# Cross-attention with a mixture of experts: clearing, query projection and two loads in another order

## The chip, the cores and the metric

The kernel runs on one core of one Trainium2 chip. The metric is the device time of one execution in microseconds (us), from the first to the last instruction of the core. Each kernel is run several times and the median is compared. The execution that the profiler recorded is one more run, and its own time stands below.

## The reference

For each of 32 batches, 100 query tokens attend to 1,444 context rows of 128 numbers, with 16 heads of 8 numbers each. The result is added to the tokens, and then each token goes through the best two of eight experts. The mask holds only ones.

```
x    = x + attention(layernorm(x), ctx, ctx, mask, W_q, W_k, W_v, W_o)     # x [32,100,128], ctx [32,1444,128]
       scores = clip(q @ k.T / sqrt(8), -50, 50);  p = exp(scores);  out = (p @ v) / sum(p)
x    = x + sum over the best 2 of 8 experts of weight * (gelu(layernorm(x) @ w1[e]) @ w2[e])
```

All of it is in float32.

## The kernel before

**Stages.** There is a start, 32 batches of attention, and a stage for the experts. The batches 0 and 1 are written out, the batches 2 to 29 are a loop over pairs (`Fori(1, B // 2 - 1)`, an even batch and then an odd one), and the batches 30 and 31 are written out again. Every engine has its own program with its own loop, so each pair ends on every engine with a branch.

**A batch.** The scores of a batch are made in 20 chunks of 3 or 2 units (a unit is 128 context rows of one group of four heads, 128x400 numbers). In a chunk TensorE (PE) multiplies `k_stack` by `q_stack` into PSUM (`score_chunk`, L816), ScalarE (ACT) takes exp (L1058), VectorE (DVE) clips (L1214), and PE later multiplies the values by the probabilities (`weigh_values`, L828). The chunks alternate between two areas of PSUM, so the scores of chunk c + 1 wait for the exp of chunk c - 1. The tables `STEP_AT` and `HALF_AT` say behind which chunk each other step stands: the next batch's keys (L747) and values (L756), and the steps of the batch before towards the experts. In chunk 15 PE does 24 multiplications in a row with the values, 48 rows of the trace under L828; this piece of each batch (x48) serves below as a mark for the length of a batch.

**Stacked keys and queries.** Keys and queries are split into a high and a low part (`k_hi`, `k_lo`, `q_parts`) and spread over the partitions by DMAs between SBUF places: `k_stack` in thirds of four DMAs of 256 KB, from SyncE's queue (SP, L509), `q_rep` and `q_stack` in DMAs of 50 KB, in the start from ACT's queue too. `q_stack` holds zeros between its blocks, which GpSimd (POOL) writes once (L641).

**The start.** DVE and POOL normalise the first four batches of x; PE turns the first context and these tokens, projects the first third of the keys (`first_key(0)`), then the queries (`project_q`), then the other keys and the values. DVE splits the queries ahead of the keys. The first scores wait for all of `q_stack` and for the first third of `k_stack`.

**Loads from HBM.** x comes in three parts (`X_PARTS`); the last, 16 batches in 1,600 rows of 512 bytes, is issued by ACT at the end of the start. A context is loaded by `load_blocks(b, p)` (L979) on ACT's queue: 128 partitions times 45 rows of 128 bytes, 5,760 small rows, 720 KB, into one of two buffers; four more rows come from SP. DVE turns a context for the next batch in three pieces behind chunks 0, 7 and 11 (`turn_keys`, L1145). There are 30 of these loads. Each stands at the head of `attend` on ACT, ahead of the batch's first exp:

```
def attend(b, p):
    if not (isinstance(b, int) and b + 2 >= B):
        ...
        load_blocks(b + 2, p)
    for c in range(CHUNKS):
        act.wait_ge(scores_ready, CHUNKS * b + c + 1)
```

[...] The functions, with the line numbers of the profile:

Of the kernel before, what the change touches and what calls it, by code (L numbers as in the profile page):

```python
# [48 lines left out]
def xattn_moe(nc, x, ctx, mask, W_q, W_k, W_v, W_o, gate_w, w1, w2, out):  # L49
    B, SQ, D = x.shape  # L50
# [21 lines left out]
    KSTEPS = TILES // KC  # L72
# [46 lines left out]
    TURN_AT = [0, 7, 11]  # L119
    WEIGHED = 5  # L120
    SPLIT_AT = 15

    ALONE = [("value", k) for k in range(KSTEPS)]

# [13 lines left out]
    FIRST_STEPS = [[s for _, s in steps] for steps in PLANS]  # L138
# [3 lines left out]
    X_PARTS = [slice(0, QB), slice(QB, 4 * QB), slice(4 * QB, B)]  # L142
# [5 lines left out]
    def is_first(b):  # L148
        return isinstance(b, int) and b < 2
# [4 lines left out]
    def scratch_step(b, n):  # L154

        return ITS_BASE[b] + n if is_first(b) else len(STEPS) * b + BEFORE + n
# [8 lines left out]
    def planned(b, c):  # L165

        if is_first(b):
            return [(FIRST_STEPS[b][n], n) for n in range(len(PLANS[b])) if FIRST_AT[b][n] == c]
        last = isinstance(b, int) and b == B - 1
        steps = [n for n in range(len(STEPS)) if STEP_AT[n] == c and (not last or IN_LAST[n])]  # L170
        return [(STEPS[n], sum(IN_LAST[:n]) if last else n) for n in steps]
# [16 lines left out]
    def turns_before(b):  # L188

        return KSTEPS * (b - 1) if not isinstance(b, int) or b >= 2 else 0  # L190
# [9 lines left out]
    def later(b, least=1):  # L200

        return not isinstance(b, int) or b >= least
# [7 lines left out]
    with es:  # L210
        def sb(name, shape, dt=F32):
            return es.enter_context(nc.sbuf_tensor(name, shape, dt))
# [4 lines left out]
        def sem(name):  # L217
            return es.enter_context(nc.semaphore(name))
# [3 lines left out]
        x_all = sb("x_all", [SQ, B, D])  # L222
# [107 lines left out]
        x_loaded = [sem(f"x_loaded{h}") for h in range(3)]  # L330
# [3 lines left out]
        ctxT_ready = sem("ctxT_ready")  # L334
# [28 lines left out]
        scratch_filled = sem("scratch_filled")  # L363
# [71 lines left out]
        def score_banks(c):  # L435

            first = SB0 * (c % 2)
            return scores[:, first:first + UNITS[c], 0:GQ]

        def probs_of(c):  # L440

            first = FIRST_UNIT[c] % RING_UNITS
            return probs[:, first:first + UNITS[c], :]
# [172 lines left out]
        def _(pool):  # L616
# [15 lines left out]
            def invert_deviations(r):  # L632
                part = slice(r * QB, (r + 1) * QB)
                pool.wait_ge(moments_ready, r + 1)
                nc.gpsimd.tensor_scalar(rstd[:, part], moments[:, part, 1], EPS, None, ALU.add).then_inc(var_ready, 1)
                pool.wait_ge(var_ready, r + 1)
                nc.gpsimd.tensor_tensor(rstd[:, part], rstd[:, part], half[:, part], ALU.pow).then_inc(rstd_ready, 1)

            invert_deviations(0)
            for p in range(2):  # L640
                nc.gpsimd.memset(q_stack[p][:].bitcast(F32), 0.0).then_inc(q_stack_cleared, 1)  # L641
            pool.wait_ge(ctx_turned, KSTEPS)
            nc.gpsimd.memset(ctx_cols[0][:, WHOLE * Q:BLOCKS * Q], 0.0).then_inc(spare_keys_cleared[0], 1)
            invert_deviations(1)
# [17 lines left out]
            for r in range(DVE_NORMS, QSTEPS):  # L662
                invert_deviations(r)
                pool.wait_ge(rstd_ready, r + 1)
                for j in range(QB):
                    b = r * QB + j
# [71 lines left out]
        def _(pe):  # L738
# [7 lines left out]
            def project_k(into, k):  # L746
                return nc.tensor.matmul(into[:, 0:KEYS[k]], w_turned[:, WK, :], ctxT[:, KEY_COLS[k]],  # L747
                                        start=True, stop=True)

            def project_q(into):  # L750
                return nc.tensor.matmul(into[:, 0:NQ], w_turned[:, WQ, :], xT, start=True, stop=True)  # L751
# [96 lines left out]
            turn_tokens(o_sum, 0).then_inc(xT_in_psum, 1)  # L848
            turn_rows(scores[:, 2, :], 0, 2).then_inc(ctx_turned, 1)
            pe.wait_ge(w_turned_ready, 1)  # L850

            def first_key(k):

                pe.wait_ge(ctxT_ready, k + 1)
                project_k(scores[:, FIRST_KEYS_IN[k], :], k).then_inc(keys_projected, 1)

            first_key(0)
            pe.wait_ge(xT_ready, 1)
            project_q(scores[:, 1, :]).then_inc(q_in_psum, 1)
            first_key(1)  # L860
            first_key(2)
            for step, (name, k) in enumerate(ALONE):
# [113 lines left out]
        def _(act):  # L976
            def load_blocks(b, p):

                act.dma_start(ctx_cols[p][:, 0:WHOLE * Q].rearrange("p (t d) -> p t d", d=Q),  # L979
                              ctx[b, 0:WHOLE * Q, :].rearrange("(i t) (g d) -> g i t d", t=WHOLE, d=Q)  # L980
                              ).then_inc(ctx_loaded[p], 16)
# [54 lines left out]
            for step, (name, k) in enumerate(ALONE):  # L1036
# [4 lines left out]
                                   ).then_inc(scratch_emptied[step % 2], 1)  # L1041
                if k == 0:
                    first_stack()
            act.dma_start(x_all[:, X_PARTS[2], :], x[X_PARTS[2]].rearrange("b q d -> q b d")).then_inc(x_loaded[2], 16)

            def attend(b, p):
                if not (isinstance(b, int) and b + 2 >= B):
                    if later(b, 2):
                        act.wait_ge(ctxT_ready, turns_before(b) + KSTEPS)
                    elif b == 1:  # L1050
                        act.wait_ge(scratch_filled, scratch_step(0, FIRST_STEPS[0].index(("turn", KSTEPS - 1))) + 1)
                    load_blocks(b + 2, p)
                for c in range(CHUNKS):
                    act.wait_ge(scores_ready, CHUNKS * b + c + 1)
                    if later(b) or c >= RING:

                        act.wait_ge(pv_done, HALVES * b + 2 * last_tile_under(c) + 2)
                    nc.scalar.activation(probs_of(c), score_banks(c), ACT.Exp, scale=SCALE).then_inc(exp_ready, 1)  # L1058
                    for (name, k), n in planned(b, c):
                        take(name, k, b + 1, b - 1, scratch_step(b, n), scratch_use(b, n)[0])  # L1060
                    if c == GATED + 2 and later(b):
                        second_share(b - 1)

            attend(0, 0)
            attend(1, 1)
            with act.Fori(1, B // 2 - 1) as i:
                attend(2 * i, 0)
                attend(2 * i + 1, 1)
            attend(B - 2, 0)
            attend(B - 1, 1)  # L1070
            for n, (name, k) in enumerate(FINISH):
# [35 lines left out]
        def _(dve):  # L1107
# [30 lines left out]
            def turn_keys(i, p, b, k):  # L1138

                if k == 0:  # L1140
                    dve.wait_ge(ctx_loaded[1 - p], 16 * (i + 1 + p))
                    dve.wait_ge(ctx_over_loaded[1 - p], 16 * (OVER * (i + p) + 1))
                dve.wait_ge(scratch_filled, value_turned(b - 1, k) + 1)
                cols = slice(KEY_BLOCKS[k].start * Q, KEY_BLOCKS[k].stop * Q)
                nc.vector.transpose(ctxT[:, cols], ctx_cols[1 - p][:, cols]).then_inc(ctxT_ready, 1)  # L1145
# [165 lines left out]
            def attend(i, p, b):  # L1311
                for c in range(CHUNKS):
# [10 lines left out]
                    for k in range(KSTEPS):  # L1323
                        if c == TURN_AT[k] and later(b) and not (isinstance(b, int) and b + 1 >= B):
                            turn_keys(i, p, b, k)
                    if c == SPLIT_AT and not (isinstance(b, int) and b + 2 >= B):
                        split_queries(b + 2)
# [137 lines left out]
```

## Time and profile before

| | |
|---|---|
| median of 3 runs | 1036.55 us (1033.01 to 1038.11) |
| the profiled execution | 1029.2 us, its span 1027.4 us |
| busy: PE, DVE, ACT, POOL | 93%, 79%, 70%, 33% of the span |
| the chain that ended last | PE 88%, DMA 2%, ACT 2%, issue 2%, SP's queue 2%, DVE 1%, POOL 1%, ACT's queue 1% |
| mean granted clock of TensorE | 0.969 of full speed |

The busy shares are averages over stages. The chain is followed back from the last instruction to what released each step, so a row of it is time that the end waited for. "ACTq" and "SPq" are the sequencers of ACT and SP, where a DMA is issued; a row there is the time that the issue held the sequencer, not the transfer. The timeline's bracket behind a row is how long the engine sat idle before it, and what ended that.

### The profile page before, as it was taken

Reading aid. Unit: us, or ns where it says so; the run is one execution under the profiler, and the core shown is the slowest. Engines: PE = TensorE matmul, PEld = TensorE weight load, DVE = VectorE, ACT = ScalarE, POOL = GpSimd, SP = SyncE. Lnnn points to the kernel's source line nnn. Section 1 sums busy time; section 2 is a strip of 40 time slices with the busy share of each in tenths; the row PEclk is TensorE's granted clock in tenths of the full one; section 3 lists DMA queues with packets and bytes.
Section 4 is the critical chain, followed back from the end, with each engine's and each line's share of the span. In section 5 each row is a group of like instructions: output and inputs, shape, how many; then the busy total and the mean of one; then the engine's idle time right before and its main releaser. Section 6 shows DMA issues by size and latency. Waiting matters only on the chain.

```text
span 1027.4 us, 31365 instructions
## 1 busy us (share of the span) xinstructions
PE 953.8 (93%) x9974; PEld 695.5 (68%) x9975; DVE 808.5 (79%) x2140; ACT 716.0 (70%) x941; POOL 340.0 (33%) x422
## 2 busy tenths in 40 slices
PE   3799999999999999999999999999999996599980
PEld 2566666666666666666666666666666773599980
DVE  5477888888888888888888888888888985444433
ACT  2577878787878787878787878787878774244430
POOL 3182322222222222222222222222222234255554
PEclk9699999999999999999999999999999999699995
DMA  6755666666666666666666666666666663122216
GB/s 182 182 150 173 186 189 188 186 188 189 186 188 186 189 187 189 186 189 188 187 186 189 186 189 186 189 186 187 189 188 186 184 229 86 41 66 67 66 43 191
DMA packets 312438, 172.70 MB, mean 168 GB/s; under 512 B 205274, under 2 KB 260518, under 8 KB 312406
## 3 DMA queue, kind: packets, MB, share of 16 engines
q1 hardware_dynamic: 131898, 142.19, 42.4%
q10 hardware_dynamic: 175612, 23.48, 14.5%
q0 software_dynamic: 4896, 6.63, 2.1%
q8 instruction: 17, 0.28, 0.1%
q14 instruction: 15, 0.12, 0.0%
HBM read 36.83 MB, written 22.08 MB: 57 GB/s over the span
## 4 chain that ended last, share of the span: by engine, by line
PE 88%; DMA 2%; ACT 2%; issue 2%; SPq 2%; DVE 1%; POOL 1%; ACTq 1%; POOLq 0%; DVEq 0%
PE scores L816 32%; PE o_sum L828 28%; PE scratch L747 7%; PE scratch L756 7%; PE scores L940 5%; PE scores L951 5%; ACT probs L1058 2%; SPq L604 1%; DMA q_stack<-q_rep 1%; ACTq L979 1%; PE scratch L794 1%; DMA x_all<-in_x_dram 1%; PE scratch L751 0%; DMA q_and_ctx<-expert_outputs 0%; POOL rows L688 0%
## 5 line engine op out<-in xcount | busy, mean ns | idle before, releaser
L1058 ACT ACTIVATE probs<-scores 128x800 f32<-128x800 f32 (+1 forms) x640 | 603.8, 973 | 152.2 <-PE scores L816 139.8
L816 PE MATMUL scores<-q_stack,k_stack 128*128 128x400 f32 x1536 | 412.9, 385 | 15.2 <-DMA q_stack<-q_rep 9.2
L1214 DVE TENSOR_SCALAR probs<-probs 128x800 f32<-128x800 f32 (+1 forms) x640 | 402.4, 661 | 16.9 <-ACT probs L1058 11.8
L816 PEld LDWEIGHTS scores<-q_stack,k_stack 128*128 128x128 f32 x1536 | 250.8, 190 | 140.8 <-ACT probs L1058 84.1
L828 PE MATMUL o_sum<-probs,v_both 128*17 128x200 f32 x6144 | 304.0, 335 | 0.0
L828 PEld LDWEIGHTS o_sum<-probs,v_both 128*17 128x17 f32 x6144 | 158.4, 97 | 109.3 <-issue 39.9
L699 POOL DMA_INDIRECT expert_rows<-rows,row_atu x64 | 71.9, 1124 | 322.0 <-DVE row_atu L1301 290.2
L756 PE MATMUL scratch<-w_turned,ctxT 128*128 128x128 f32 x768 | 101.0, 275 | 0.0
L756 PEld LDWEIGHTS scratch<-w_turned,ctxT 128*128 128x128 f32 x768 | 99.7, 191 | 0.7 <-issue 0.3
L747 PE MATMUL scratch<-ctxT,w_turned 128*128 128x512 f32 x186 | 85.3, 567 | 0.0
L1154 DVE COPY v_both<-scratch 128x512 f32<-128x512 f32 x93 | 63.7, 685 | 20.4 <-PE scratch L756 20.4
L725 POOL DMA_INDIRECT expert_outputs<-ctx_nat,tile_home x57 | 55.7, 977 | 64.4 <-DVE ctx_nat L1415 61.7
L688 POOL TENSOR_SCALAR rows<-token,moments,rstd 100x128 f32<-100x128 f32 x64 | 70.7, 1107 | 6.9 <-POOL rstd L684 6.9
L682 POOL TENSOR_SCALAR rstd<-moments 100x1 f32<-100x1 f32 x32 | 32.3, 1011 | 114.7 <-DVE moments L1254 114.6
L1018 ACT COPY k_full<-scratch 128x512 f32<-128x512 f32 (+1 forms) x93 | 52.1, 561 | 19.2 <-PE scratch L747 14.3
L1118 DVE TENSOR_TENSOR k_lo<-k_full,k_hi 128x512 fp32r<-128x512 f32 (+1 forms) x93 | 61.5, 662 | 3.2
L940 PE MATMUL scores<-ctxT 128*128 128x128 f32 x456 | 62.2, 281 | 0.0
L951 PE MATMUL scores<-w_sb,k_full 128*128 x456 | 61.6, 279 | 0.0
L1088 ACT ACTIVATE k_full<-scores 128x512 f32<-128x512 f32 x57 | 34.1, 598 | 38.6 <-PE scores L940 38.0
L940 PEld LDWEIGHTS scores<-ctxT 128*128 128x128 f32 x456 | 57.1, 197 | 0.3 <-issue 0.2
L1116 DVE CAST k_hi<-k_full 128x512 fp32r<-128x512 f32 (+1 forms) x93 | 38.0, 409 | 24.3 <-ACT k_full L1018 24.2
L951 PEld LDWEIGHTS scores<-w_sb,k_full 128*128 128x128 f32 x456 | 56.3, 194 | 0.3 <-issue 0.2
(148 smaller groups left out, 665.7 us busy)
## 6 DMA issues: line engine op xcount, KB each, us to landing
k_stack<-k_hi SPq DMA_DIRECT2D x192, 256.0 KB, 3.5
k_stack<-k_lo SPq DMA_DIRECT2D x192, 256.0 KB, 4.8
expert_rows<-fill SPq DMA_DIRECT2D x32, 406.2 KB
q_and_ctx<-in_ctx_dram ACTq DMA_DIRECT2D x15, 720.0 KB
ctx_nat<-in_ctx_dram ACTq DMA_DIRECT2D x15, 720.0 KB
q_rep<-q_parts SPq DMA_DIRECT2D x126, 50.0 KB
q_stack<-q_rep SPq DMA_DIRECT2D x126, 50.0 KB, 2.6
v_both<-expert_rows SPq DMA_DIRECT2D x57, 65.0 KB, 1.8
```

The costliest lines, as they stand in the source:

```text
L688: ins = nc.gpsimd.tensor_scalar(rows[:, k, TOKEN:D], token[:], moments1[:, 0:1], rstd1[:, 1:2], ALU.subtract, ALU.mult)
L699: nc.gpsimd.indirect_dma_start(out=expert_rows[0:E * CAP, :], out_offset=bass.IndirectOffsetOnAxis(ap=row_atu[:, k:k + 1], axis=0), in_=ro ...
L747: return nc.tensor.matmul(into[:, 0:KEYS[k]], w_turned[:, WK, :], ctxT[:, KEY_COLS[k]], start=True, stop=True)
L756: last = nc.tensor.matmul(scratch[:, j * P:(j + 1) * P], ctxT[:, t * P:(t + 1) * P], w_turned[:, WV, :], start=True, stop=True)
L816: last = nc.tensor.matmul(score_banks(c)[:, m, :], k_stack[p][:, g, t * P:(t + 1) * P], q_stack[p][:, :, g, :], start=True, stop=True)
L828: last = nc.tensor.matmul(sums_of(g, s), v_ones[p][:, t, 2 * g + s, :], probs[:, u, s * PQ:(s + 1) * PQ].rearrange("p (h q) -> p h q", h=2 ...
L940: last = nc.tensor.matmul(hidden_in[n % 2][:, c * P:(c + 1) * P], w1_tile[:, n % 2, c * P:(c + 1) * P], tileT[:, n % 2, :], start=True, st ...
L951: last = nc.tensor.matmul(y_in[n % 2], hiddenT[:, n % 2, c, :], w2_sb[:, bass.ds(expert, 1), c, :].rearrange("f o d -> f (o d)"), start=(c ...
L1058: nc.scalar.activation(probs_of(c), score_banks(c), ACT.Exp, scale=SCALE).then_inc(exp_ready, 1)
L1118: nc.vector.tensor_tensor(k_lo[:, cols], k_full[:, k, 0:KEYS[k]], k_hi[:, cols].bitcast(F32), ALU.subtract).then_inc(k_split, 1)
L1154: nc.vector.tensor_copy(v_ones[p][:, k * KC:(k + 1) * KC, :, 0:2 * DH], scratch[:, bank, :].rearrange("p (t n d) -> p t n d", t=KC, n=PAIR ...
L1214: nc.vector.tensor_scalar(chunk, chunk, LOW, HIGH, ALU.max, ALU.min).then_inc(probs_ready, 1)
```

## The change

- POOL clears both `q_stack` buffers before it inverts the first deviations, not after.
- PE projects the first queries ahead of the first third of the keys. It waits for a second copy of context (`ctxT_ready` 2) first, since the queries go into the PSUM bank that this copy reads.
- ACT issues the last part of x and the load of the third context (number 2) behind the exp of chunk 3 in batch 0, not before batch 0.
- The loads at the head of each batch are gone. Behind the exp of chunk 14, batch b now loads context b + 3 into the buffer that batch b has just turned; it waits for that batch's third turn (in batch 0 for the last turn in PSUM).
- ACT's loop is one pair shorter, and batches 28 and 29 are written out on ACT.
- DVE waits for the four extra rows of a context ahead of the third turn, not of the first.

```
+    LOAD_AT = 14
+    LATE_X_AT = 3
...
-            invert_deviations(0)
             for p in range(2):
                 nc.gpsimd.memset(q_stack[p][:].bitcast(F32), 0.0).then_inc(q_stack_cleared, 1)
+            invert_deviations(0)
...
             pe.wait_ge(w_turned_ready, 1)
+            pe.wait_ge(ctxT_ready, 2)
...
-            first_key(0)
             pe.wait_ge(xT_ready, 1)
             project_q(scores[:, 1, :]).then_inc(q_in_psum, 1)
+            first_key(0)
...
-            act.dma_start(x_all[:, X_PARTS[2], :], x[X_PARTS[2]].rearrange("b q d -> q b d")).then_inc(x_loaded[2], 16)
...
             def attend(b, p):
-                if not (isinstance(b, int) and b + 2 >= B):
-                    if later(b, 2):
-                        act.wait_ge(ctxT_ready, turns_before(b) + KSTEPS)
-                    elif b == 1:
-                        act.wait_ge(scratch_filled, scratch_step(0, FIRST_STEPS[0].index(("turn", KSTEPS - 1))) + 1)
-                    load_blocks(b + 2, p)
                 for c in range(CHUNKS):
...
                     nc.scalar.activation(probs_of(c), score_banks(c), ACT.Exp, scale=SCALE).then_inc(exp_ready, 1)
+                    if not later(b) and c == LATE_X_AT:
+                        act.dma_start(x_all[:, X_PARTS[2], :], x[X_PARTS[2]].rearrange("b q d -> q b d")).then_inc(x_loaded[2], 16)
+                        load_blocks(2, 0)
+                    if c == LOAD_AT and not (isinstance(b, int) and b + 3 >= B):
+                        if later(b):
+                            act.wait_ge(ctxT_ready, turns_before(b + 1) + KSTEPS)
+                        else:
+                            act.wait_ge(scratch_filled, scratch_step(0, FIRST_STEPS[0].index(("turn", KSTEPS - 1))) + 1)
+                        load_blocks(b + 3, 1 - p)
...
-            with act.Fori(1, B // 2 - 1) as i:
+            with act.Fori(1, B // 2 - 2) as i:
                 attend(2 * i, 0)
                 attend(2 * i + 1, 1)
+            attend(B - 4, 0)
+            attend(B - 3, 1)
...
                     dve.wait_ge(ctx_loaded[1 - p], 16 * (i + 1 + p))
+                if k == KSTEPS - 1:
                     dve.wait_ge(ctx_over_loaded[1 - p], 16 * (OVER * (i + p) + 1))
```

On POOL in the start, before and then after the change (`rstd` is the inverted deviation, `q_and_ctx` holds the first context buffer):

```order
L628 AFFINE_SELECT ident<-ident 128x128
L635 TENSOR_SCALAR rstd<-moments 100x4
L637 TENSOR_TENSOR rstd<-rstd,half 100x4
L641 MEMSET q_stack 128x1600 x2
L643 MEMSET q_and_ctx 128x32
```

```order
L630 AFFINE_SELECT ident<-ident 128x128
L642 MEMSET q_stack 128x1600 x2
L637 TENSOR_SCALAR rstd<-moments 100x4
L639 TENSOR_TENSOR rstd<-rstd,half 100x4
L645 MEMSET q_and_ctx 128x32
```

The two memsets moved ahead of the two operations on `rstd`.

On ACT from the end of the start to chunk 5 of batch 0, before and then after (each ACTIVATE is the exp of one chunk; the copy into `ctxT` belongs to chunk 3):

```order
L1039 COPY v_both<-scratch 128x32x16 x2
L1044 DMA x_all<-in_x_dram 100x16x128
L979 DMA q_and_ctx<-in_ctx_dram 128x45x32
L1058 ACTIVATE probs<-scores 128x1200
L1058 ACTIVATE probs<-scores 128x800
L1058 ACTIVATE probs<-scores 128x1200
L1058 ACTIVATE probs<-scores 128x800
L1014 COPY ctxT<-scratch 128x512
L1058 ACTIVATE probs<-scores 128x1200
```

```order
L1042 COPY v_both<-scratch 128x32x16 x2
L1054 ACTIVATE probs<-scores 128x1200
L1054 ACTIVATE probs<-scores 128x800
L1054 ACTIVATE probs<-scores 128x1200
L1054 ACTIVATE probs<-scores 128x800
L1056 DMA x_all<-in_x_dram 100x16x128
L982 DMA q_and_ctx<-in_ctx_dram 128x45x32
L1017 COPY ctxT<-scratch 128x512
L1054 ACTIVATE probs<-scores 128x1200
```

The two loads moved from ahead of the first exp to between the fourth and the fifth, ahead of a copy.

On ACT at the entry of the loop before the change, and then behind chunk 14 of the loop's even batch after it (the last ACTIVATE of the first fence is chunk 0, the first of the second is chunk 14):

```order
L1058 ACTIVATE probs<-scores 128x800
L1066 UNCONDITIONAL_BRANCH
L1066 ISA
L979 ISA
L979 DMA q_and_ctx<-in_ctx_dram 128x45x32
L1054 ISA
L1057 ISA
L1058 ACTIVATE probs<-scores 128x1200
```

```order
L1054 ACTIVATE probs<-scores 128x1200
L1060 REGISTER_ALU
L982 ISA
L982 DMA ctx_nat<-in_ctx_dram 128x45x32
L1011 REGISTER_ALU
L1020 REGISTER_ALU
L1021 COPY k_full<-scratch 128x512
```

The load moved from between the last exp of one batch and the first of the next to between the exp of chunk 14 and the copies of the next batch's keys.

## Rows read from the trace of the kernel before

**Rows 1.** Chain in order of time, the start: start us, us, what.

```profile
9.42 3.39 DVE probs L1183 x4
...
13.99 1.05 PE scores L747 x2
...
19.61 0.61 SPq L509
...
20.98 8.47 DMA q_stack<-q_rep
```

**Rows 2.** Timeline of POOL and DVE: start us, us, engine, line, operation [idle before].

```profile
8.00 0.24 POOL L635 TENSOR_SCALAR rstd<-moments 100x4 f32<-100x4 f32 x1 [5.52 <-DVE moments L1176]
...
9.35 2.79 POOL L641 MEMSET q_stack<- 128x1600 f32 x2
...
23.28 1.15 DVE L1183 TENSOR_SCALAR w_sb<-x_all,moments,rstd 100x128 f32<-100x128 f32 x4 [0.31 <-POOL rstd L637]
```

**Rows 3.** Page, DMA issues: times, KB each, median us to landing.

```profile
k_stack<-k_lo SPq DMA_DIRECT2D x192, 256.0 KB, 4.8
```

**Rows 4.** Timeline of ACT and its queue, start and batch 0.

```profile
20.66 0.70 ACTq L1044 DMA_DIRECT2D x_all<-in_x_dram  x1
...
21.39 3.55 ACTq L979 DMA_DIRECT2D q_and_ctx<-in_ctx_dram  x1
...
37.18 0.59 ACT L1014 COPY ctxT<-scratch 128x512 f32<-128x512 f32 x1 [1.58 <-PE scratch L742]
...
54.61 1.17 ACT L1058 ACTIVATE probs<-scores 128x1200 f32<-128x1200 f32 x1 [0.38 <-PE scores L816]
```

**Rows 5.** One window: us, busy PE, PEld, DVE, ACT, POOL, PEclk, DMA, GB/s.

```profile
25.20:41.50 16.30, 9.54 (x35) 7.17 (x39) 6.98 (x25) 6.73 (x9) 2.06 (x3) 0.50 0.85 210
```

**Rows 6.** Timeline of ACT and PE's weight loads, into an even batch.

```profile
556.03 0.56 ACTq L979 DMA_DIRECT2D q_and_ctx<-in_ctx_dram  x1
556.78 3.25 ACT L1058 ACTIVATE probs<-scores 128x1200 f32<-128x1200 f32 x3 [0.47 <-issue]
...
558.00 0.48 PEld L816 LDWEIGHTS scores<-q_stack,k_stack 128*128 128x128 f32 x3 [0.45 <-ACT probs L1058]
```

**Rows 7.** Chain in order of time: x48 of batches 18, 19, 20, 29, 30.

```profile
525.43 2.15 PE o_sum L828 x48
...
550.90 2.15 PE o_sum L828 x48
...
576.77 2.16 PE o_sum L828 x48
...
807.77 2.15 PE o_sum L828 x48
...
833.03 2.15 PE o_sum L828 x48
```

**Rows 8.** Timeline of SP's queue and ACT, into an odd batch.

```profile
529.84 0.62 SPq L509 DMA_DIRECT2D k_stack<-k_hi  x1
...
530.00 0.84 ACT L1058 ACTIVATE probs<-scores 128x800 f32<-128x800 f32 x1 [0.16 <-PE scores L816]
...
530.15 0.55 ACTq L979 DMA_DIRECT2D ctx_nat<-in_ctx_dram  x1
```

**Rows 9.** Timeline of DVE, ACT and PE's weight loads, chunk 14 of batch 19.

```profile
546.09 0.64 DVE L1145 STREAM_TRANSPOSE ctxT<-q_and_ctx 128x448 f32<-128x448 f32 x1
...
548.45 1.18 ACT L1058 ACTIVATE probs<-scores 128x1200 f32<-128x1200 f32 x1 [0.60 <-PE scores L816]
549.66 1.21 ACT L1018 COPY k_full<-scratch 128x512 f32<-128x512 f32 x2
...
550.47 0.14 PEld L798 LDWEIGHTS scratch<-ident,rows 100*128 100x128 f32 x1
```

**Rows 10.** DMA view, packets on ACT's queue (q10): 530.2 to 553.9, then 31 to 60.

```profile
q10 hardware_dynamic: 5764, 0.74, 19.8%
...
q10 hardware_dynamic: 5843, 0.77, 18.5%
```

## The prediction

> **What bounds the kernel now.** I read the chain that ended last first: 88% of it is PE, so a change elsewhere helps only where the chain leaves PE. It leaves it in two places that this change touches. The first is the start. In the chain in order of time [rows 1] the normalisation on DVE takes 3.39 us, and a DMA into `q_stack` takes 8.47 us and ends at 29.45; only then do the first scores begin. The window behind it [rows 5] shows what that idle time leaves: from 25.2 to 41.5 us TensorE's granted clock was 0.50, the lower of its two levels, 1.2 GHz, and PE was busy for 9.54 of 16.3 us. The second place is the step from one batch into the next. From x48 to x48 [rows 7] the step into batch 19 costs 25.47 us, into batch 20 25.87, and into batch 30, where ACT issues no load and no loop branches, 25.26. So each even step has 0.61 us too much and each odd one 0.21, and the timeline shows where: ACT's first exp of batch 20 was ready but came 0.47 us late for "issue", and PE's weights waited 0.45 us for that exp [rows 6].
>
> My sum is made against the profiled execution's own 1029.2 us (span 1027.4, and 1.8 around it). The median shown is 1036.55, which is 7.3 more; I take the sum off the median.
>
> **The change part by part.**
>
> *POOL's clearing.* Four normalisations took 3.38 us in the start and 1.15 later, with the same shapes [rows 2]; only the first four lie beside the memsets of 9.35 to 12.14. The memsets move into POOL's idle 5.52 us ahead of 8.00, which covers their 2.79, and the `rstd` steps are not delayed. Gain on the chain: 3.39 - 1.15 = 2.2 us. Without that cover, `rstd` would be late by up to 2.8 and the gain gone.
>
> *Queries first.* The first key piece, 1.05 us on PE [rows 1], leaves the queries' path. PE now waits for the copy of the turned tokens, which that piece had covered, but PE turns the last context rows meanwhile. The added wait for the second context copy costs nothing: ACT makes that copy ahead of the tokens' copy, for which PE waits anyway; the keys and values queue behind both. The keys now end 1.05 behind the queries, but DVE splits the queries first, as before, so not all of the 1.05 is lost to the keys; I take a gain of 0.4 for them (bounds 0 and 1.05). SP's issues, the key thirds and then `q_stack`, come 2.2 + 0.4 = 2.6 earlier.
>
> *The two loads out of the start.* They leave ACT's queue at 20.66 and 21.39 [rows 4], beside the 8.47 us transfer. What lands last then? The fourth DMA of the key third was issued at 19.61 [rows 1], now at 17.0, and takes a median 4.8 us [rows 3]: 21.8. `q_stack` goes out at 18.4 and has one third ahead of it, as always. I take 21.9 in place of 29.45: **-7.5 us**, of which 2.6 is from the earlier issues. The landing could stay at 8.47 if the key thirds and not the loads hold it (-2.6), or follow the issue in 2.6 (-8.5); I take nearly the shorter, since the loads are the only traffic there that other landings don't have.
>
> *The same loads in batch 0.* Now ACT's sequencer issues them between two exps. The one took 0.70 and the other 3.55 [rows 4], 4.3 together. In the trace ACT was free from 35.60 (37.18 less 1.58) until PE's turned context came; the issues start while the exp of chunk 3 runs, about 0.8 earlier (an exp of two units takes 0.84 [rows 8]), so they end near 39.1 on the old clock face and hold the copy and the exp of chunk 4 by **+1.9 us**. Bounds: nothing, if the second issue needs only the 0.55 of the loop [rows 8], since 1.3 is covered; 4.3, if nothing is. The part of x is asked for by DVE five chunks later; if it were late, the clips and then PE's values would wait.
>
> *The fourth context.* Chunk 14 of batch 0 stands at 54.61, some 20 us behind the exp of chunk 3 [rows 4], and there ACT issues the next load on a queue that holds x and the third context. A context in the loop is all moved between 530.2 and 553.9, 5,764 packets [rows 10], 23.7 us; x has to go ahead of it. So the issue meets a queue that is not empty. It need not wait for the landing: the issue at 21.39 got through by 24.94, though the 5,843 packets of 31 to 60 us [rows 10] are the context's 5,760 and 83 others, so x still moved then. I take **+2.0 us**, bounds 0 and 9 (the context's 23.7 and for x about 5, an estimate from the 3.55 for which it held the next issue, against 20). Behind it on ACT stand the copies of two key thirds, and behind these PE's later steps of the chunk.
>
> Start together: -7.5 + 1.9 + 2.0 = **-3.6 us**.
>
> *The loads at chunk 14 in the loop.* Into batch 20 ACT branches and issues for 0.56 us, and the exp comes 0.47 late [rows 6]; without the issue the branch ends under the exp of chunk 19, and PE gets back its 0.45. Even steps in the loop: 14 (batches 2 to 28), 6.3 us. Into an odd batch the issue of 0.55 lies under the exp of 0.84 [rows 8]; what it costs is within the 0.21 of that step, and I take 0.15, as the loop's register instructions have a share. Odd steps: 15 (batches 1 to 29), 2.2 us. Together **-8.5**; bounds -3.5 (even 0.25, odd 0) and -11.7 (0.61 and 0.21 in full).
>
> At chunk 14 I cost the issue at nothing. What hides it is the exp of 1.18 us that starts at 548.45; the copies follow at 549.66 [rows 9], and an issue of 0.55 is over by then. The wait in front of it is for the third turn, which ends at 546.73, 1.7 us before. If that cover failed, the first copy would end 0.55 later than about 550.27, and PE, which loads the next weights at 550.47, would wait. The transfer itself keeps its pace of one per batch and lands earlier than it is needed.
>
> *The rest.* DVE's moved wait releases a turn that waited for nothing in the trace; nothing. Two more batches written out on ACT save one branch, too little to count.
>
> Sum: -3.6 - 8.5 = **-12 us**, from 1029.2 to 1017 in a profiled run and from 1036.55 to **1024.5** in the median.
>
> **The rivals.**
>
> *A, the start gives nothing back.* The issues in batch 0 cost only their covered 0.7 and 0.55, and PE's shorter idle time leaves the clock at its upper level. For it: an issue alone takes 0.55. Against: 3.55 was measured behind this very load of x, and PE still idles before the first scores. Then -7.5 - 8.5, and up to 2 of the half-clock stretch (at the upper level its 9.54 us of PE would be 4.8, most of it beside ACT's exps): about 1018.5 to 1020.5.
>
> *B, the start gives all back.* The issue at chunk 14 of batch 0 waits until the third context has nearly landed, +7 rather than +2: start +1.4, sum -7, 1029.5. For it: 20 us are less than the transfers need. Against: x had not landed when the issue behind it got through.
>
> *C, the branch stays.* PE's and ACT's branches alone hold the even step, and the loop gains 3.5: -7, 1029.5. For it: the even step's excess has both causes mixed. Against: the row names ACT's issue as what PE's weights waited for.
>
> *D, slower.* The issue at chunk 14 does not fit under the exp. In each of 29 batches (0 to 28) the copies, the next exp and PE come 0.55 later: +16, sum +4, 1040.5. It decides from 0.41 us a batch on. Against it: an issue of ACT at 530.15 took the usual 0.55 although SP issued from 529.84 to 530.46 [rows 8]. The Trainium skill (Perfetto Trace Analysis, section DMA Instruction — HWDGE (DVE, Sync)) says that an issue first locks a descriptor generator that the issuing sequencers share and holds it until all its descriptors are made, which would speak for D where SP's issues meet chunk 14; by that rule one issue of SP in the way would add about 0.6 a batch, an estimate. The row at 530.15 does not show such a lock; the 3.55 behind x may.
>
> **How the numbers follow.** Under or over by 0.5%, 5.2 us, is about what this measurement can tell from no change, so faster means below 1031.4. Chances: my forecast (1020.5 to 1028.5) 0.50, A 0.14, B 0.22, C 0.08, D 0.06. The forecast and A are faster; so are some 0.7 of B and C, which end near the border; the rest of them and a milder D are the same. Faster 0.83, same 0.12, slower 0.05. The range reaches from A's clock case to B and C: 1017 to 1031.
>
> **What would show it.** In the profile after: four normalisations in about 1.2 us near 9.4; first scores near 22; the two issues behind the fourth exp and the time that they take; how long the issue at chunk 14 of batch 0 takes; no "issue" wait ahead of the first exp of an even batch, and periods from x48 to x48 near 25.3 for odd and 25.4 for even batches; copies of the keys right behind the exp of chunk 14. I would be wrong if the loop's issue stretched beyond that exp (D), if batch 0 grew by more than 4 us, or if the first scores stayed later than 25.

## The result

| | before | after |
|---|---|---|
| median of 4 runs each | 1037.33 us (1033.01 to 1041.27) | 1065.26 us (1060.1 to 1065.89) |
| ratio, with its 95% interval | | 1.026 (1.021 to 1.031): slower |
| the profiled execution, its span | 1029.2, 1027.4 us | 1060.1, 1058.3 us |
| busy: PE, DVE, ACT, POOL | 93%, 79%, 70%, 33% | 91%, 76%, 67%, 31% |
| mean granted clock | 0.969 | 0.960 |

The change costs 28 us in the median, 31 in the profiled executions. In the changed kernel L982 is `load_blocks`, L1021 the copy of a key third, L818 the scores, L830 the values (x48), L1054 the exp.

The start up to the first scores went as forecast. Timeline of PE in the changed kernel, first for the start, then around chunk 14 of batch 14:

```profile
22.01 1.15 PE L818 MATMUL scores<-q_stack,k_stack 128*128 128x400 f32 x5 [2.84 <-DMA q_stack<-q_rep]
...
437.19 0.43 PE L800 MATMUL scratch<-ident,rows 100*128 100x100 f32 x1 [3.85 <-ACT k_full L1021]
437.55 3.55 PE L830 MATMUL o_sum<-probs,v_both 128*17 128x200 f32 x48
...
464.22 2.23 PE L830 MATMUL o_sum<-probs,v_both 128*17 128x200 f32 x48
```

The first scores stand at 22.01; `q_stack` had held them until 29.45 [rows 1]. But at 437.19 PE waits 3.85 us for ACT's copy of a key third, a wait that the kernel before does not have. ACT's timeline names the cause; in it "issue" is idle time that no wait in the profile explains, and the ACTq row just ahead shows ACT's sequencer held for that time:

```profile
26.14 0.32 ACTq L1056 DMA_DIRECT2D x_all<-in_x_dram  x1
26.48 3.34 ACTq L982 DMA_DIRECT2D q_and_ctx<-in_ctx_dram  x1
...
29.86 0.59 ACT L1017 COPY ctxT<-scratch 128x512 f32<-128x512 f32 x1 [2.50 <-PE scratch L744]
...
48.56 1.17 ACT L1054 ACTIVATE probs<-scores 128x1200 f32<-128x1200 f32 x1 [0.39 <-PE scores L818]
48.56 5.84 ACTq L982 DMA_DIRECT2D ctx_nat<-in_ctx_dram  x1
54.50 1.00 ACT L1021 COPY k_full<-scratch 128x512 f32<-128x512 f32 x2 [4.77 <-issue]
...
430.98 1.17 ACT L1054 ACTIVATE probs<-scores 128x1200 f32<-128x1200 f32 x1 [0.61 <-PE scores L818]
431.21 5.17 ACTq L982 DMA_DIRECT2D ctx_nat<-in_ctx_dram  x1
436.55 1.00 ACT L1021 COPY k_full<-scratch 128x512 f32<-128x512 f32 x2 [4.41 <-issue]
...
514.42 0.55 ACTq L982 DMA_DIRECT2D q_and_ctx<-in_ctx_dram  x1
515.41 1.14 ACT L1021 COPY k_full<-scratch 128x512 f32<-128x512 f32 x2
...
573.54 1.90 ACT L1054 ACTIVATE probs<-scores 128x800 f32<-128x800 f32 x2 [0.17 <-PE scores L818]
```

The last row holds the step into batch 20 (the exps of chunks 19 and 0, without a gap): the 0.47 for "issue" of [rows 6] is gone. But the same issue now takes 0.55 us in one batch and 5.17 in another. Where it is short, the copies follow the exp at once, as the prediction had it; where it is long, they wait 4.41. The waits of the whole changed kernel (total, times, longest):

```profile
DVE k_hi L1123 <- ACT k_full L1021: 53.6, 60, 5.0
...
ACT k_full L1021 <- issue: 27.0, 7, 4.8
...
PE scratch L800 <- ACT k_full L1021: 19.7, 8, 4.2
...
PE scores L818 <- DMA k_stack<-k_lo: 6.3, 6, 2.5
```

A second wait is new as well: six times PE's scores wait for the stacked keys. And the idle time has an echo in the clock. Windows of batch 14 (columns as in [rows 5]):

```profile
431.00:433.30 2.30, 2.30 (x9) 1.19 (x7) 1.32 (x3) 1.15 (x1) 1.70 (x2) 1.00 0.99 338
433.30:437.20 3.90, 0.05 (x2) 0.01 (x1) 0.03 (x1) 0.65 (x2) 0.00 (x0) 0.96 0.22 71
437.20:441.20 4.00, 4.00 (x50) 2.10 (x51) 3.54 (x8) 2.30 (x4) 0.00 (x0) 0.61 0.68 152
441.20:447.00 5.80, 5.80 (x56) 5.09 (x60) 4.79 (x22) 4.68 (x7) 0.00 (x0) 1.00 1.06 278
```

PE stands still for 3.9 us, and in the 4.0 behind that the granted clock is 0.61, a stretch that lies partly at the lower level (0.5 of full speed, 1.2 GHz) and partly at the upper: the x48 took 3.55 us where that of the next batch took 2.23. So a held issue like this one costs about 3.9 + 1.3 = 5.2 us, spread over two steps.

From the x48 of batch 0 to that of batch 31 the changed kernel needs 889.45 - 55.99 = 833.5 us, the kernel before 857.74 - 57.52 = 800.2. The step into batch 1, behind the load at chunk 14 of batch 0, takes 33.07 (30.51 before). Of the others, six take 28.4 to 29.8 us, ten 26.3 to 27.1 (a shorter hold, or the slow x48 and late keys behind a long one); the undisturbed ones from batch 4 on take 25.3 to 25.9, and the step into batch 2 takes 26.28 in both kernels.

Why is the queue not empty? The DMA view of the changed kernel for the load issued at 514.42 (queue, packets, MB, share of 16 engines), for 517 to 522, 522 to 528 and 528 to 539 us; q1 is SP's queue, q10 ACT's:

```profile
q1 hardware_dynamic: 579, 1.05, 68.8%
q10 hardware_dynamic: 1248, 0.16, 23.3%
...
q1 hardware_dynamic: 1075, 1.32, 68.8%
q10 hardware_dynamic: 290, 0.04, 4.4%
...
q10 hardware_dynamic: 3813, 0.49, 28.2%
q1 hardware_dynamic: 812, 0.57, 19.0%
```

From 517.21 on SP issues the key thirds 1 and 2, and then the queries. Beside these the context's rows move at 1248/5 = 250, then at 290/6 = 48 packets per us; from 528 on, where smaller transfers lie beside them, at 3813/11 = 347. All 5,764 packets take from 517.1 to 544.5. In the kernel before, the rows of a load issued at 530.15 began at 532.5, when most of the thirds had passed, and were over at 553.6 [rows 8, 10]. So this transfer ends 30 us after its issue, and the next issue comes after 26: it meets rows of the transfer before. In the changed kernel an issue that met 123 packets (at 405.72) took 0.56; at 431.21 it met 520 and was let go when 102 were left; at 673.41 it met 442, took 5.46, and was let go at 103. From chunk 14 of batch 0 on, all ten long issues of this kernel met some 145 packets or more, and no short one met more than 123. Yet the number alone does not decide: in `e2` below, one that met some 230 took 0.56, and one that met 201 took 1.85.

### The profile page after: what moved, and what is told of

Read it like the earlier page. It is cut to its first block and busy times, and to the rows that moved or that the text cites. A ratio compares the mean times of both kernels' runs of the same rounds, so it can differ in the third digit from the quotient of the medians.

```text
span 1058.3 us, 31338 instructions
## 1 busy us (share of the span) xinstructions
PE 963.7 (91%) x9974; PEld 702.3 (66%) x9975; DVE 808.0 (76%) x2140; ACT 711.6 (67%) x941; POOL 332.9 (31%) x422
## 5 line engine op out<-in xcount | busy, mean ns | idle before, releaser
L1054 ACT ACTIVATE probs<-scores 128x800 f32<-128x800 f32 (+1 forms) x640 | 600.4, 973 | 161.6 <-PE scores L818 159.6
L818 PE MATMUL scores<-q_stack,k_stack 128*128 128x400 f32 x1536 | 408.8, 384 | 14.5 <-DMA k_stack<-k_lo 6.3
L818 PEld LDWEIGHTS scores<-q_stack,k_stack 128*128 128x128 f32 x1536 | 252.7, 190 | 134.2 <-ACT probs L1054 71.2
L830 PE MATMUL o_sum<-probs,v_both 128*17 128x200 f32 x6144 | 313.4, 342 | 0.0
L830 PEld LDWEIGHTS o_sum<-probs,v_both 128*17 128x17 f32 x6144 | 161.5, 99 | 114.0 <-issue 50.7
L1021 ACT COPY k_full<-scratch 128x512 f32<-128x512 f32 (+1 forms) x93 | 51.1, 562 | 45.4 <-issue 27.0
```

Source lines behind the costliest of these rows:

```text
L818: last = nc.tensor.matmul(score_banks(c)[:, m, :], k_stack[p][:, g, t * P:(t + 1) * P], q_stack[p][:, :, g, :], start=True, stop=True)
L830: last = nc.tensor.matmul(sums_of(g, s), v_ones[p][:, t, 2 * g + s, :], probs[:, u, s * PQ:(s + 1) * PQ].rearrange("p (h q) -> p h q", h=2 ...
```

## The experiments

Theory 1: at chunk 14 the transfer starts beside the key thirds, lasts longer than a batch, and the next issue then holds ACT. Rival 2: the backlog comes from the start. Rival 3: the issue is slow by itself or through SP's issues, whatever is in the queue. Rival 4: the transfer slows the keys, and PE waits for these. Rival 5, of the later runs: the key third has no slack, so what the context gains the keys lose. Each ratio is against the kernel before, run beside it on the same chip.

**The start alone** (`e1`, and again as `e14`). The loads stand at the head of the batch again:

```
             def attend(b, p):
+                if not (isinstance(b, int) and (b == 0 or b + 2 >= B)):
...
+                    load_blocks(b + 2, p)
                 for c in range(CHUNKS):
...
-                    if c == LOAD_AT and not (isinstance(b, int) and b + 3 >= B):
...
-                        load_blocks(b + 3, 1 - p)
```

> Only the start of the change: POOL's clearing first, the queries first, x and the third context behind the exp of chunk 3 in batch 0; from batch 1 on the loads stand at the head of the batch again. Theory 1 (the queue: the load at chunk 14 takes longer than a batch, so that the next issue holds ACT): the start is not to blame, the first scores stand near 22 us, no issue of a load takes over 1 us from batch 1 on, and the time is about 6 us under the kernel before, ratio 0.994. Rival 2 (the late x and third context begin the backlog, and the loop only inherits it): issues of 2 us and more return in the loop, and the time is 10 us or more over the kernel before.

Ratio 0.988 (0.979 to 0.997), profiled 1027.5; no issue from batch 1 on is over 0.62. The start alone brings a gain; rival 2 falls with this and with `e2` below, which has the loss without the new start. One step took 28.14 us, into batch 22, where DVE waited 2.9 for a context. The repetition:

> The start alone once more, beside the two with the earlier fill: ratio 0.985 to 0.992 if its first measurement (0.988) held. What the fill is worth is the difference to the kernel with the earlier fill at the head of the batch.

Ratio 0.989 (0.984 to 0.994), profiled 1021.9, without such a step. At the x48 of batch 1 (88.03 in the kernel before) `e1` stands at 81.36 and `e14` at 80.24, so the start is worth 6.7 and 7.8 us there. In the medians it is 9 to 12, since the profiled execution of the kernel before, 1029.2, was faster than any other of its runs here. The changed kernel, with the same start and a load at chunk 14 of batch 0, stands at 89.06: by these executions that load costs 7.7 and 8.8 us, all that the start had gained.

**The order alone** (`e8`): POOL's clearing and the queries as changed, both loads of the start ahead of batch 0 as before.

> Only POOL's clearing first and the queries ahead of the first keys; x and the third context are issued ahead of batch 0 and all loads at the head of the batch, as in the kernel before. By the prediction's split of the start: the four normalisations shrink from 3.4 to 1.2, all issues come 2.6 earlier, but the last DMA into q_stack still takes about 8.5 us, and the first scores stand at 27 (29.69 in the kernel before, 22.0 in the changed one). If the order alone made the gain: first scores near 22 to 23. If it gives nothing: 29 or more.

One execution: 1027.39 us. PE's timeline:

```profile
27.68 2.00 PE L818 MATMUL scores<-q_stack,k_stack 128*128 128x400 f32 x5 [9.09 <-DMA q_stack<-q_rep]
```

In the kernel before this row stands at 29.69, in the changed one at 22.01. By these three executions the order gave 2.0 of the 7.7 us, and the two loads that no longer lie beside `q_stack` gave 5.7. But in `e2`, whose start is that of the kernel before, the row stands at 31.66. So the large part, of the loads, is clear, and the 2.0 of the order is no larger than what two executions of one start differ by.

**The loop alone** (`e2`): the start of the kernel before, with the loads at chunk 14. Against the kernel before:

```
+                    if c == LOAD_AT and not (isinstance(b, int) and b + 3 >= B):
...
+                        load_blocks(b + 3, 1 - p)
```

> Only the loop of the change: the loads behind the exp of chunk 14, three ahead; the start is that of the kernel before. Theory 1 (the queue): some 8 to 10 issues in the loop take 1.2 to 5.5 us and the time is 20 to 35 us over the kernel before, ratio 1.02 to 1.034. Rival 2 (a backlog begun in the start): the loop runs without long issues, and the time is some 8 us under the kernel before, ratio 0.992. Rival 3 (every issue at chunk 14 costs its own 0.55, however short): about +16 - 8 = 8 us over, evenly in all batches, ratio 1.008.

Ratio 1.026 (1.016 to 1.037): the loss is all here. But only five issues took over 1.2 us, 1.85 to 4.90, all up to 462 us. After that every issue took 0.56, and still every second step from 521.29 to 825.73 took 29.1 to 31.4 us. The waits show the other form of the loss:

```profile
PE scores L817 <- DMA k_stack<-k_lo: 19.6, 10, 3.1
...
ACT k_full L1019 <- issue: 10.1, 3, 4.1
```

Here rival 4 has a part: the context or the key thirds come late, and which of the two varies from batch to batch.

**A smaller load, and smaller key thirds** (`e3`, `e7`): both are the changed kernel with one of the two colliding transfers cut. The first line is from `e3`, the others are from `e7`; from batch 4 on `n` is 2, half of the partitions.

```
+                rows = WHOLE if isinstance(b, int) and b < 4 else 36
...
+                n = 4 if isinstance(b, int) and b < 4 else 2
...
-                    sp.dma_start(k_stack[p][t:P:4, :, cols].bitcast(F32),
-                                 part[:, cols].bitcast(F32)).then_inc(k_stacked[k], 16)
+                    sp.dma_start(k_stack[p][t:P:4, 0:n, cols].bitcast(F32),
+                                 part[0:32 * n, cols].bitcast(F32)).then_inc(k_stacked[k], 16)
```

> The changed kernel, but from context 4 on a load brings 36 rows a partition in place of 45 (the last fifth of those rows is left out of the load, so the values are not the reference's; all other work is the same). Theory 1 (the queue): a transfer of about 30 us becomes one of about 24, shorter than a batch of 25.4; no issue from batch 2 on takes over 0.7 us, and the time falls from 1060 to between 1015 and 1025 in a profiled run, ratio to the kernel before 0.985 to 0.995. Rival 3 (the issue at chunk 14 is held by SP's issues or by its own cost, whatever is still in the queue): the issues stay long in every third or fourth batch, and the time stays over 1045, ratio over 1.012. Rival 4 (the transfer slows the stacking of the keys, and PE waits for that): a gain of no more than a fifth of the loss, 1053 or more.

> The changed kernel, loads behind chunk 14 with all their 45 rows, but from batch 4 on each stacking DMA of the keys moves half as much (128 of 256 KB: the second half of its partitions is left out, so the scores are not the reference's; instructions and issues are the same in number). Theory 1 (the transfer of the context is slow because it lies beside the key thirds): from batch 4 on a context is all moved in less than a batch, issues take 0.56, PE's scores don't wait for keys; 1015 to 1022 profiled, ratio 0.985 to 0.993. Rival 3 (the number of SP's issues beside it, not their bytes, holds ACT's issue): long issues stay, ratio over 1.015.

With 36 rows no issue from batch 1 on took over 0.58, which speaks against rival 3; but the time fell only to 0.998 (0.994 to 1.003), not to 0.985 to 0.995, since PE's scores still waited 13.8 us for key thirds, in 8 waits of up to 4.3. With half the key bytes everything is as the prediction wanted it: 0.986 (0.979 to 0.994), and the loop's steps are 25.3 and 25.5 from batch 4 on. The issues of this kernel by buffer (min/median/max in ns, first and last start):

```profile
L983 ACTq DMA_DIRECT2D q_and_ctx<-in_ctx_dram x15: 554/555/2654, 26.0 to 747.5; - x15
L983 ACTq DMA_DIRECT2D ctx_nat<-in_ctx_dram x15: 554/555/6116, 46.7 to 772.6; - x15
```

The two maxima are those of batch 0, where the keys were not halved; all others are 0.55 to 0.58 at the place where the changed kernel's were long. SP issues as often as before, so its number of issues isn't what holds ACT.

The changed kernel's own trace says so too. SP's queue around the hold of 431.21 to 436.38:

```profile
430.79 0.66 SPq L511 DMA_DIRECT2D k_stack<-k_lo  x1
438.35 0.54 SPq L511 DMA_DIRECT2D k_stack<-k_hi  x1
```

SP issues nothing from 431.45 to 438.35, while ACT's issue is held. Of the nine issues over 1.2 us in this kernel's loop (1.25 to 5.46) none has more than 0.73 us of SP's issuing beside it, and two, at 379.64 and 592.19, have none. So rival 3 falls. The lock of a shared descriptor generator, which the Trainium skill describes (Perfetto Trace Analysis, section DMA Instruction — HWDGE (DVE, Sync)) and which the prediction named for rival D, is not what this trace shows for these holds.

**Another place in the batch** (`e4`, `e5`, `e6`): the start of the change, with loads behind the exp of chunk 0 (two ahead), 18 or 19 (three ahead).

```
-    LOAD_AT = 14
+    LOAD_AT = 18
```

> The start of the change, and the loads two ahead as in the kernel before, but behind the exp of chunk 0 in place of ahead of it (ACT's loop has its old length). Theory 1 (the queue): the transfer keeps the place in the batch where it ends before the next issue, no issue takes over 0.7 us, and the issue is now covered by an exp of 1.18 us: start -6 and loop -8, 1013 to 1018 in a profiled run, ratio 0.984 to 0.99. If the issue is no part of the wait at the step into a batch (the branch holds it alone): the loop gains nothing, -6, ratio 0.994. If the later phase of 1.3 us is enough to bring the transfer past the next issue: long issues come back, ratio over 1.0.

> The changed kernel with the load three ahead behind the exp of chunk 18 in place of 14. Theory 1 (what matters is where in the batch the transfer starts: behind the key thirds it keeps ahead of the next issue, beside them it doesn't): at chunk 18 most of thirds 1 and 2 have been issued, the issue meets few rows of the transfer before, hardly any issue takes over 1 us, DVE never waits for a context, and the time is 1012 to 1020 in a profiled run, ratio 0.985 to 0.992. Rival 4 (any load three ahead crosses the keys and makes PE's scores wait for the key thirds): PE's scores wait for key thirds in many batches and the ratio stays over 1.005.

> The same behind the exp of chunk 19, the last of the batch: on ACT the load then stands just ahead of the loop's branch, where it stood just behind it before the change. Theory 1: transfers as in the kernel before, no issue over 1 us; the sum of issue and branch on ACT at an even step is what it was, so the loop gains nothing (periods 25.48 and 25.88) and only the start's gain remains: 1022 to 1026 profiled, ratio 0.99 to 0.995. If the place before the branch already hides the issue: even periods 25.5, ratio 0.985 to 0.988. Rival 4: ratio over 1.005.

Behind chunk 0: 0.997 (0.992 to 1.002). Most steps are 25.32 (odd) and 25.47 (even), 0.16 and 0.41 less than before, so the forecast gain of the loop is there; but five steps take 27.7 to 32.3. DVE's waits for a context in this kernel:

```profile
DVE ctxT L1151 <- DMA q_and_ctx<-in_ctx_dram: 12.2, 3, 5.7
...
DVE ctxT L1151 <- DMA ctx_nat<-in_ctx_dram: 9.7, 3, 4.9
```

Issued one exp later, the transfer's end reaches the next key thirds and lands too late: the load issued at 189.32 moved its last row at 220.9, with SP's issues of thirds 1 and 2 from 209.79 on. None of the three cases of the expectation had this. Behind chunk 18: 0.986 (0.974 to 0.998); four issues in the loop took 1.5 to 2.7 us, and DVE waited 15.9 us in 5 waits, which the expectation had ruled out; the ratio came out as it said, the profiled 1030.17 (1012 to 1020 expected) did not. Behind chunk 19: 0.988 (0.984 to 0.992), steps 25.48 and 25.82, so the sum of issue and branch is what it was, and one late context (5.1 us).

**The key third held back** (`e9` at chunk 18, `e10` at 14, `e11` at 0): SP waits for the context before it issues the next key third.

```
+                if not (isinstance(b, int) and b + 2 >= B):
+                    sp.wait_ge(ctx_loaded[p], 16 * (i + 2))
                 stack_keys(1 - p, b + 1)
```

> The changed kernel with the load behind chunk 18 and one wait more: SP issues the first key third of the next batch only when the context that is under way has landed. Theory 1 (the end of the transfer is slow because the key third is put beside it): the last tenth of the context moves as fast as the rest, a context is in some 18 us after its first row, the next issue meets an empty queue in every batch, DVE waits for no context, and the loop keeps 25.3 and 25.5 in all batches: 1010 to 1017 in a profiled run, ratio 0.975 to 0.984, with little spread. Rival 5 (the key third has no slack: what the context gains, PE's scores lose): PE waits for the key third at the head of the batches, ratio 0.99 to 1.01. If the end of the transfer is slow by itself: as with chunk 18 alone, spikes of 2 to 5 us remain.

> The changed kernel as it is, loads behind chunk 14, with the same wait of SP for the context ahead of the first key third. Theory 1: the transfer still starts beside key thirds 1 and 2, which takes 13 us for its second to fifth tenth, but its last tenth is free: about 25.5 us in all, near the length of a batch, so long issues become few, and SP's third comes some 4 us later: ratio 0.985 to 1.005. Rival 3 (the issue at chunk 14 is held by something else than the transfer before): long issues stay as they were, ratio over 1.02.

> The start of the change, loads two ahead behind the exp of chunk 0, with the same wait of SP for the context ahead of the first key third. Theory 1: no context is late any more for DVE, the five steps of 27 to 32 us that this placing had without the wait are gone, periods 25.3 and 25.5 throughout: 1012 to 1018 profiled, ratio 0.975 to 0.985. Rival 5 (no slack for the key third): PE's scores wait for keys, ratio 0.99 or more.

Ratios 1.088 (1.083 to 1.094), 1.077 (1.070 to 1.083) and 1.065 (1.059 to 1.071). Rival 5 is right, and its price was far too low. The issues in the loop are short now (0.62 at most, but for one of 0.82 in `e10`), but PE pays. Waits of `e9`:

```profile
PE scores L820 <- DMA k_stack<-k_lo: 89.2, 20, 9.9
```

In `e9` SP waited 28 times for a context, 189.7 us in all and up to 7.7, and the key thirds have no such slack.

**The fill moved** (`e12` at chunk 18, `e13` at the head): SP's fill of the expert rows at the head of its batch.

```
+                fill_rows(b + 1)
                 stack_queries(1 - p, b + 1)
...
-                fill_rows(b + 1)
                 stack_keys(1 - p, b + 1)
```

> The changed kernel with the load behind chunk 18, and SP issues the fill of the expert rows (406 KB, 800 rows of 520 bytes) at the head of its batch, ahead of the query stack, in place of just ahead of the first key third. Theory 1 (the end of the transfer is slowed by the bytes put beside it): beside the middle of the context the fill costs it nothing, the key third starts to move some 2 us earlier and ends earlier, and the context ends 1 to 2 us earlier; the three issues over 2 us and the late contexts of chunk 18 alone become none or one: 1012 to 1018 profiled, ratio 0.978 to 0.985. If the fill only changes places with the key third, which then meets the context 2 us earlier: the spikes stay or grow, ratio 0.985 to 1.0. If the fill delays the query stack: PE waits for it at the head of each batch, ratio over 1.0.

> The start of the change, loads two ahead at the head of the batch as in the kernel before, and the same earlier fill. The loop's periods stay 25.48 and 25.88 with no late context: 1020 to 1023 profiled, ratio 0.985 to 0.989, and a smaller spread than that of the start alone. If the fill brings nothing there: ratio 0.988 and one step of 28 to 32 us in some runs.

Ratios 1.089 (1.082 to 1.095) and 1.086 (1.080 to 1.091): wrong in size and sign. In `e13` the issues at the head of the batch, 0.55 in the kernel before, now took up to 12 us, and DVE waited 81.8 us for contexts. From 584 to 588 us the queues moved this:

```profile
q1 hardware_dynamic: 1212, 0.91, 76.5%
q10 hardware_dynamic: 208, 0.03, 4.3%
```

208/4 = 52 context packets per us, the pace that the changed kernel had beside the thirds. But near 545 the kernel before moved the same fill beside the context without harm (831 packets in 2 us). So it is not simply the bytes beside it that make the pace fall. Nor is it full DMA engines alone: in the changed kernel the rows moved at 144/3 = 48 per us from 522 to 525, with a DMA share of 1.06, and at 146/3 = 49 from 525 to 528, with a share of 0.44. Why they go at about 50 is not settled.

## Why the prediction was wrong

**The step that failed** is in the loop: "At chunk 14 I cost the issue at nothing", with its reason, "The transfer itself keeps its pace of one per batch and lands earlier than it is needed." The cover of 1.18 us that it named exists, and an issue of 0.55 fits under it. But the pace was read from a transfer that started at 530.15, behind the key thirds [rows 10], and taken along to a start beside them. There it needs some 30 us, 4 to 5 more than a batch; the next issue is held until about 100 packets are left, or the keys come late. From the x48 of batch 1 to that of batch 31 the kernel lost 30.7 us where 8.5 were to be gained, so instead of nothing the place cost about 39 us. `e2` shows the loss without the new start, `e3` that the hold goes with a shorter transfer, `e7` that all of the loss goes with lighter key thirds.

**The fourth context** was the same error in batch 0: +2.0 forecast, 7.7 and 8.8 us measured (beside `e1` and `e14`), with 4.77 us of idle time on ACT and an x48 of 4.20 us behind it. So at the x48 of batch 1 the changed kernel stood 1.0 us behind the kernel before, where -3.6 was forecast. The bound of 9 was good, the value taken was not, and the reasoning ("20 us are less than the transfers need") had already been written down under rival B. For the loop the same comparison was not made: the 23.7 us of [rows 10] against a batch of 25.5 left a margin of only 1.8.

**What held.** The four normalisations take 1.12 us (1.15 forecast). First scores at 22.01 (21.9), and with the order alone 27.68, so the split of -7.5 into 2.6 and 4.9 is not contradicted (2.0 and 5.7, single executions). The two issues behind chunk 3: the exp of chunk 14 in batch 0 starts at 48.56 in place of 54.61 [rows 4], 6.05 earlier (7.5 - 1.9 = 5.6 forecast; the whole start without the fourth context is worth 6.7 and 7.8 in `e1` and `e14`). The even and odd steps where nothing collides: 0.41 and 0.16 shorter in `e4` and `e7` (0.45 and 0.15). The two gains were sized about rightly, and the sum had the wrong sign for two terms on the other side, one taken at nothing and one at 2.0. That the start alone comes out at the ratio that was forecast for the whole (1024.5/1036.55 = 0.988) is luck: the forecast had the loop's 8.5 in it.

**The rivals.** D named the place, the issue at chunk 14 that does not fit, and a loss; its mechanism (0.55 in each of 29 batches) and price (+16) were wrong: most issues still took 0.55 to 0.6, and the others up to 5.46, because of rows left in ACT's own queue. B was right about batch 0, in mechanism and size (+7 said, 7.7 and 8.8 measured), but it had the loop gain its 8.5. Against C the prediction said that [rows 6] names ACT's issue; the row names ACT's exp, and that exp's "issue" covers the branch as well. `e4` settles it: with the issue under an exp and the branch as before, the even step is 0.41 shorter. A does not matter beside these.

The version to keep is the start of the change without its loop: 0.988 and 0.989 in two measurements. Chunk 18 or 19 is no better than that within the intervals.

## What to carry to other kernels

When a transfer is moved, read its duration again at the new place: list what the other queues move in the window into which it goes, and what pace the same queue had in a window of that kind. For a transfer that recurs, compare that duration with the period. Here, once it was longer, the backlog came out as a held issue, as a late landing, or as lateness of the traffic beside it, and taking away one of these forms alone moved it to another (`e3`, `e9` to `e11`). A short issue can be counted on to hide under a short instruction only when its queue is empty.

## What the hardware showed

- From batch 1 on, in every run, an issue of 5,760 rows that met an empty queue took 0.62 us or less. In the changed kernel it still took 0.56 with 123 packets of the load before in the queue, but with 442 or 520 it held ACT's sequencer for over 5 us, until 103 and 102 were left. In other runs the border lay elsewhere (some 230 packets met and 0.56 us in `e2`).
- Rows of 128 bytes moved at 347 packets per us over 11 us, and at 48 to 49 beside the key thirds, both with the DMA engines full (share 1.06, 522 to 525) and with a share of 0.44 (525 to 528).
- 3.9 us of an idle PE were followed by a stretch at a granted clock of 0.61, which cost another 1.3 us on the x48 (3.55 in place of 2.23).
